# Cross attention in a two-layer transformer kernel: softmax rows divided before they are turned, values as the stationary operand in 32-column quarters, the output arriving transposed

## The reference

```
q = LN(x) @ Wq.T + bq;  k = ctx @ Wk.T + bk;  v = ctx @ Wv.T + bv      # heads of 32
s = (q_h @ k_h.T * tau + delta) / sqrt(32)                             # 128 rows x 77, per head
p = softmax(s);  o_h = p @ v_h;  x = x + concat(o_h) @ Wo.T + bo
```

## Time and profile before

| | us |
|---|---|
| median of 3 runs | 4210.44 (4210.44 to 4210.71) |
| the profiled execution | 4207.2 |
| its span, first to last instruction | 4205.1 |
| stage one, about | 2190 |

### The profile page before, as it was taken

How to read it: one execution, slowest core, us unless ns; L and a number is a source line. 1 busy time by engine, 2 the same in 40 slices (tenths; PEclk the granted TensorE clock), 3 DMA queues, 4 the chain that set the end, 5 groups by cost and what they waited for, 6 DMA issues and landing times.

```text
span 4205.1 us, 51100 instructions
## 1 busy us (share of the span) xinstructions
PE 3705.1 (88%) x19906; PEld 2919.3 (69%) x19906; DVE 2283.2 (54%) x4629; ACT 1642.5 (39%) x2603; POOL 1085.5 (26%) x852
## 2 busy tenths in 40 slices
PE   6989888989878999999988999998899999978888
PEld 3867677767666777877766676766677677756666
DVE  3565656565665766667653445445455654453333
ACT  1444444444444444444423555552132222232222
POOL 1333333323222333333320222221122222250110
PEclk8989898989888999999988999999899999987879
DMA  3010100101111110111021111110022111030000
GB/s 119 24 42 22 34 29 24 39 21 41 35 43 41 42 38 30 38 41 40 31 74 34 46 43 46 53 48 33 32 78 68 58 63 43 33 121 11 21 26 11
DMA packets 106279, 180.02 MB, mean 43 GB/s; under 512 B 29598, under 2 KB 30366, under 8 KB 104504
## 3 DMA queue, kind: packets, MB, share of 16 engines
q1 hardware_dynamic: 101496, 162.07, 11.6%
q0 software_dynamic: 3968, 10.50, 0.8%
q10 hardware_dynamic: 576, 4.19, 0.3%
HBM read 106.09 MB, written 70.64 MB: 42 GB/s over the span
## 4 chain that ended last, share of the span: by engine, by line
PE 66%; DVE 14%; issue 10%; ACT 5%; POOL 3%; DMA 2%; SPq 0%; POOLq 0%; ACTq 0%; DVEq 0%
PE ps L307 11%; PE ps L309 10%; PE ps L308 10%; PE ps L302 7%; PE ps L314 7%; PE ps L522 5%; PE ps L1224 4%; PE ps L1208 3%; PE ps L511 3%; DVE st L587 2%; PE ps L1189 2%; PE ps L1754 2%; PE ps L1768 1%; DVE sTa L710 1%; DVE Sb L666 1%
## 5 line engine op out<-in xcount | busy, mean ns | idle before, releaser
L902 POOL TENSOR_TENSOR Sb<-Sb,mx 128x1232 f32<-128x1232 f32 x128 | 288.9, 2257 | 987.9 <-DVE mx L671 987.9
L522 PEld LDWEIGHTS ps<-VB,PT 103*128 103x128 f32 x3072 | 400.4, 206 | 73.7 <-ACT PT L835 57.0
L1592 POOL TENSOR_TENSOR Sw<-Sw,mw 128x2048 f32<-128x2048 f32 x64 | 233.7, 3651 | 833.0 <-DVE mw L1314 833.0
L522 PE MATMUL ps<-VB,PT 103*128 103x66 f32 x3072 | 399.3, 287 | 50.0 <-ACT PT L835 50.0
L302 PE MATMUL ps<-KB,QT 128*128 128x308 f32 x1024 | 353.1, 450 | 1.6 <-ACT QT L796 1.6
L314 PE MATMUL ps<-ident,xn 128*128 128x128 f32 x1120 | 193.4, 304 | 155.8 <-DVE xn L1271 73.3
L314 PEld LDWEIGHTS ps<-ident,xn 128*128 128x128 f32 x1120 | 151.2, 159 | 213.9 <-issue 86.4
L796 ACT ACTIVATE QT<-ps,bq 128x512 f32<-128x512 f32 x128 | 88.0, 688 | 518.9 <-PE ps L309 518.9
L835 ACT COPY PT<-ps 103x384 f32<-103x384 f32 x512 | 239.9, 480 | 95.5 <-PE ps L511 94.9
L511 PEld LDWEIGHTS ps<-ident,Sb 128*103 128x103 f32 x1536 | 214.3, 173 | 83.1 <-DVE Sb L666 35.9
L666 DVE TENSOR_TENSOR Sb<-ps,dlt 128x308 f32<-128x308 f32 x512 | 225.9, 470 | 84.5 <-PE ps L302 83.4
(11 more groups left out here) (271 smaller groups left out, 8256.0 us busy)
## 6 DMA issues: line engine op xcount, KB each, us to landing
XB<-in_x SPq DMA_DIRECT2D x16, 1024.0 KB, 5.4
x_scratch<-XB SPq DMA_DIRECT2D x16, 1024.0 KB, 4.3
XB<-x_scratch SPq DMA_DIRECT2D x16, 1024.0 KB, 5.9
x_scratch<-XB SPq DMA_DIRECT2D x64, 256.0 KB, 2.0
...
```

Source lines behind the costliest of these rows:

```text
L522: m = PE.matmul(ps[:, p, o:o + 66], PT[:, 3 * g + c, :], VB[kvi(n) % 2][:, g, c, :], start=(j == 0 and c == 0), stop=(j == 1 and c == 2), ...
L902: G.tensor_tensor(sv, sv, last(mx[:, n % 2, :], NK), ALU.subtract).then_inc(g_sub, 1)
```

## The change

Rows are divided first. A new step `norm(n)` stands one tile after `softexp(n)`: VectorE sums each head's 77 exponentials and takes the 16 reciprocals (dn), and GpSimd multiplies Sb by them, 128 x 1232. `ptrans`, `pv` and `wo` come one tile later than they did, and Sb has three buffers. `ptrans` turns head by head, four pieces of 77 columns for a group. In `pv` the values are the stationary operand, 77 rows by 32 columns, plain and without the column of ones, and the turned rows PT move, 128 columns for each head; head i of a group writes the PSUM partitions 32i to 32i+31. So the output of a tile is transposed as it arrives, one bank for 16 heads; `otrans`, On and the divisions behind `pv` are gone, and ScalarE and VectorE split this bank into OTp. `pv` waits for each group's PT copy apart. `feed` starts 39 slots after the block's first tile in place of 33, and its 17 steps take the slots 0 to 16 one after another, where they were spread over 24. VB, 103 rows of placed values, becomes VS, read back in one DMA with rows of 2 KB. The later stages get a buffer On of their own.

```diff
-FEED = (0, 2, 4, 6, 8, 10, 12, 14, 15, 16, 17, 18, 19, 20, 21, 22, 23)
+FEED = (0, 1, 2, 3, 4, 5, 6, 7, 8, 9, 10, 11, 12, 13, 14, 15, 16)
-    if p == 16 and s == 8:
+    if p == 16 and s == 14:
         new_o()
-    f, s = divmod(z - 33, 24)
+    f, s = divmod(z - 39, 24)
# walk_a
-    for n in range(2 * NT + 3):
+    for n in range(2 * NT + 4):
         if cur:
             scores(n, 0)
             scores(n, 1)
+        if p1:
+            norm(n - 1)
         if p2:
-            otrans(n - 2)
-        if p1:
-            ptrans(n - 1, 0)
+            ptrans(n - 2, 0)
...
-            wo(n - 2)
+            wo(n - 3)
...
-            pv(n - 1, 0)
+            pv(n - 2, 0)
# TensorE
             def ptrans(n, g):
                 p = take("PT", n, g)
-                pe.wait_ge(a_exp, n + 1)
-                for c in range(3):
-                    o = 308 * g + OFF3[c]
-                    m = PE.transpose(ps[0:103, p, 128 * c:128 * c + 128], Sb[:, n % 2, o:o + 103], ident[:, :])
+                pe.wait_ge(g_norm, n + 1)
+                for i in range(4):
+                    o = NK * (4 * g + i)
+                    m = PE.transpose(ps[0:NK, p, 128 * i:128 * i + 128], Sb[:, n % 3, o:o + NK], ident[:, :])
             def pv(n, f):
-                p = take("PV", n, f)
-                pe.wait_ge(a_pt, 4 * n + 4)
...
-                        m = PE.matmul(ps[:, p, o:o + 66], PT[:, 3 * g + c, :], VB[kvi(n) % 2][:, g, c, :],
-                                      start=(j == 0 and c == 0), stop=(j == 1 and c == 2), skip_group_check=True)
+                p = bank("PV", n) if f else take("PV", n)
+                for g in (2 * f, 2 * f + 1):
+                    pe.wait_ge(a_pt, 4 * n + g + 1)
+                    for i in range(4):
+                        h = 4 * g + i
+                        m = PE.matmul(ps[32 * i:32 * i + 32, p, 128 * g:128 * g + 128],
+                                      VS[:, kvi(n) % 2, 32 * h:32 * h + 32], PT[:, h, :], start=True, stop=True)
-            def otrans(n):
...
# VectorE
             def scores(n, g):
-                ve.wait_ge(pe_pt, 4 * (n - 1))
+                ve.wait_ge(pe_pt, 4 * (n - 2))
+            def norm(n):
+                ve.wait_ge(a_exp, n + 1)
+                V.tensor_reduce(dn[:, n % 2, :], Sb[:, n % 3, :].rearrange("p (h k) -> p h k", h=16), X,
+                                ALU.add).then_inc(v_chain, vc.up())
+                V.reciprocal(dn[:, n % 2, :], dn[:, n % 2, :]).then_inc(v_den, 1)
             def pv(n, f):
-                V.reciprocal(rc[:, f, :], ov[:, :, 32]).then_inc(v_chain, vc.up())
-                V.tensor_tensor(On[:, n % 2, 256 * f:256 * f + 256].rearrange("p (h d) -> p h d", h=8),
-                                ov[:, :, 0:32], last(rc[:, f, :], 32), ALU.mult).then_inc(v_on, 1)
+                if f:
+                    ve.wait_ge(a_ohi, n + 1)
+                    V.tensor_tensor(OTp[1][:, n % 2, :, :], quad(bank("PV", n)), OTp[0][:, n % 2, :, :].bitcast(F),
+                                    ALU.subtract).then_inc(v_olo, 1)
# ScalarE
-                A.copy(PT[:, 3 * g:3 * g + 3, :],
-                       ps[0:103, bank("PT", n, g), 0:384].rearrange("p (c n) -> p c n", c=3)).then_inc(a_pt, 1)
+                A.copy(PT[:, 4 * g:4 * g + 4, :],
+                       ps[0:NK, bank("PT", n, g), :].rearrange("p (c n) -> p c n", c=4)).then_inc(a_pt, 1)
# GpSimd
+            def norm(n):
+                sv = Sb[:, n % 3, :].rearrange("p (h k) -> p h k", h=16)
+                gp.wait_ge(v_den, n + 1)
+                G.tensor_tensor(sv, sv, last(dn[:, n % 2, :], NK), ALU.mult).then_inc(g_norm, 1)
# SyncE
-                for c, k, k0, n, r0, c0 in SEGS:
-                    SY.dma_start(VB[s][r0:r0 + n, :, c, c0:c0 + 33],
-                                 Vd[L, b].rearrange("(g i) k e -> i k g e", i=4)[k, k0:k0 + n]).then_inc(ld_VB[s], 16)
+                SY.dma_start(VS[:, s, :], Vd[L, b]).then_inc(ld_VS[s], 16)
```

122 lines of the change are left out of this document (50 added, 72 removed).

## The result

The changed kernel takes 4109.9 us (4104.2 to 4120.3, 4 runs) against 4210.6 (4210.4 to 4212.3, 4 runs): ratio 0.9767, 95% interval 0.9744 to 0.9791. The forecast was 4082. The profiled execution took 4104.2 us, its span is 4102.1; the forecast for it was 4079.

The account below looks back on a forecast made before the run. TensorE was taken to bound five of eight tile kinds, VectorE two, first-layer A a ScalarE-VectorE chain. First layer -98, second -35, +5 gave 4079 profiled, 4082 median; own range 4020 to 4140 (53%), whole range 3965 to 4190.

Parts of the forecast that it names:

- pv: TensorE's weighted sums: quarters run side by side, 1.7 us a tile, saving 0.9; bounds 1.3 and 3.5 to 3.9.
- The cancelling turns: TensorE, each tile: 16 head-by-head turns in place of 12 add 0.44 us, the dropped turns of On save 0.47.
- VectorE, +0.39 net: Each tile: divisions and reciprocals removed, 1.25 us; sum 1.44 and reciprocal 0.20 added; on the path in second-layer A and B.
- C and D of the second layer, 0.9 off each: Second-layer tiles bound by TensorE: C falls to 14.7 us and D to 13.9.
- The second layer's sum, -35: Second-layer round of four tiles falls 2.2 us to 53.8; 16 rounds give -35 us.
- The first layer's sum, 64.9 a round: First-layer round: C 14.7, D 19.4, B 12.8, A 18.0 us; 6.1 less, 16 rounds give -98 us.
- The feed steps: First layer: statistics (2.4 us) go B to C, one Wout product (0.9) B to A, two turns C to D.
- The forecast's A: First-layer tile A: ends near 18.0 us, from 21.47; the two ends 16.5 and 21.5.
- One load in place of six; nothing: DMA and start: one load replaces six for 16 tiles, ahead of need, so no time changes.
- +5 for the longer pipeline: Whole kernel: pipeline one tile longer, with one partly filled turn of the loop, costs 5 us once.
- half clock may turn up in the second layer: From a 13% rival at 4158 us: TensorE stays idle; each 10 us at 1.2 GHz costs up to 5.
- The serial rival: TensorE's weighted sums: quarters' weight loads do not overlap, 3.9 us a tile, +176 us, 4258 in all; chance 13%.

Follow-up runs that it names:

- sum_small: The changed kernel with VectorE's sum of exponentials cut from 16 x 77 to 16 x 2 columns: 4049.8 us, one run.
- feed_only: The kernel before with only the seventeen feed steps moved to consecutive slots from slot 39 on: 4160.3 us, ratio to before 0.9892.
- pv_one_quarter: The changed kernel with all sixteen heads' weighted sums written by one column quarter of TensorE, over each other: 4297.2 us, one run.

## Why the prediction was right, and where it was not

The time, 4109.9, lies in the range and in the forecast's own range, 28 us above 4082. That it is so near is in part luck. The first layer (tiles 0 to 64) gave 90 us of the 98 forecast, the second (64 to 127) gave 5 of 35, and the start, which was put at nothing, and the longer pipeline, which was put at +5, made up 13 of the missing 38. Its terms, in their order:

- **`pv`.** Right in mechanism, off in size: 1.01 us, not 1.7; the borders cost 0.14 in all, not 0.4. The bound of 1.3 was itself too high. The Trainium skill's rule that weight loads overlap running matmuls only where the row group differs (TensorE: Matmul & The Clock Gate, The mechanism) does not agree with the trace: all quarters use the same 77 rows and ran four abreast, and on one quarter the same passes took 3.61 us. The Trainium skill's page on tiling (TensorEngine Tiling, Key Properties), by which tiles may load and multiply in parallel, with an estimate of 0.9 us as the best case, does: the first four weight loads start 7 ns apart and run beside the matmuls.
- **The cancelling turns, ScalarE, GpSimd.** Right. The PT copy takes 581 ns (at most 640 said), the multiply is hidden, the maximum is not slowed.
- **VectorE, +0.39 net.** This is the step that failed, in "A: 13.40 + 0.39 - 0.9 out of the 1.40 wait for On: 12.9". The net of an engine's work is not the net on the path. What was removed stood in front of a wait; what was added stands behind it, and A came to 14.4. That TensorE no longer waits for On is true, and it gained nothing in a tile that VectorE ends. B's +0.5 to 0.8 is not taken apart: with the sum cut short (`sum_small`) B was no shorter.
- **C and D of the second layer, 0.9 off each.** 0.3 and 0.7 came. The saving was in fact 1.6, but the first half of `pv` is now 0.57 us long and stood as cover for the turned rows' low part: TensorE waits 0.89 us behind it in C. The forecast saw this for the `win` products in D of the first layer (1.0 said, 1.06 measured) and not for the query products.
- **The second layer's sum, -35.** In the 13 steady rounds it came to +9.6 where -2.2 a round would be -29: 38 us of error. Over the whole layer it came to -5, since tiles 64 to 72, with the last feed steps in them, gained 9 and the last tiles 5.
- **The first layer's sum, 64.9 a round.** Measured 64.9, and D is right to the digit; but C is 2.0 below its forecast and A 1.7 above. The agreement of the total is in part chance. Of C's 2.0, `pv` explains 0.7 (1.6 saved, 0.9 said) and the feed steps 0.3 (1.2 in `feed_only`, 0.9 said); what the other 1.0 is, the runs do not separate.
- **The feed steps.** Costed as work that moves from tile to tile, "the statistics leave B for C" and so on, which would sum to about zero. Alone they gave 50 of the 103 us (38.2 and 12.1). The forecast's A, and its reason that the last relus no longer stand behind an exponential, held part of this gain, but it was nowhere said to be half of the whole; and alone they gave 0.8 in A, 2.3 in B and 1.2 in C, and cost 1.5 in D.
- **"One load in place of six; nothing", and +5 for the longer pipeline.** The start gained 8.3 us. The loads were indeed hidden; the stores, which the same change of layout made whole, were not. The +5 did not show: from the last subtraction to the last output product it is 31.5 us before and 31.9 after.
- **The rivals.** That half clock may turn up in the second layer came true (0.99 to 0.91), and with it one of the forecast's own signs of being wrong. It is not what lengthened A: with the clock raised, A did not move. It goes with 0.3 to 0.6 us in some rounds of the changed kernel, and in one round it made 3 us of difference once VectorE was relieved. The serial rival did not come true; `pv_one_quarter` shows that its price was about right, 193 us against the 176 said.
